# Attention probabilities against values: eight groups of two heads in quarters of the array's columns, in place of four groups of four heads

## What is computed

```python
x = x + _L0_conv_ref(_gn(x), L0_conv_W)
x = x + _L1_conv_ref(_gn(x), w_qkv, b_qkv, rpb, w_proj, b_proj)
...
qkv = (x @ w_qkv + b_qkv).reshape(B, H, W, 3, HEADS, HEAD_DIM)   # 16 heads of 8
for a in range(7):
    for b in range(7):
        logits.append(einsum('bnhwd,bnhwd->bnhw', q, ks) + bias)   # key at the window's (a, b)
attn = softmax(stack(logits))
out = sum over the window of attn * v
return out @ w_proj + b_proj
```

## Time and profile before

| | before |
|---|---|
| median of 3 runs | 1246.21 us (1243.89 to 1247.28) |
| the profiled execution | 1245.71 us |
| its span, first to last instruction | 1243.9 us |
| mean granted TensorE clock | 0.905 of 2.4 GHz |
| busy: TensorE / VectorE / ScalarE / GpSimd | 1097.8 / 885.1 / 666.9 / 594.8 us |

### The profile page before, as it was taken

How to read it: one execution, slowest core, us unless ns; L and a number is a source line. 1 busy time by engine, 2 the same in 40 slices (tenths; PEclk the granted TensorE clock), 3 DMA queues, 4 the chain that set the end, 5 groups by cost and what they waited for, 6 DMA issues and landing times.

```text
span 1243.9 us, 33582 instructions
## 1 busy us (share of the span) xinstructions
PE 1097.8 (88%) x12452; PEld 766.3 (62%) x12452; DVE 885.1 (71%) x2137; ACT 666.9 (54%) x1874; POOL 594.8 (48%) x1279
## 2 busy tenths in 40 slices
PE   3799999946489999999999999999999999999993
PEld 3555555536257676766767666666776667677762
DVE  2522212269778888898888889887888888788881
ACT  2300000061076766868677686766768576676862
POOL 4000000050055757576575766657576665747661
PEclk7599999965588999999999999998999899899995
DMA  9400000034055767677586766757576675858661
GB/s 257 86 26 39 39 26 39 37 86 103 14 129 136 194 124 192 133 170 159 128 195 126 191 131 155 181 124 183 114 199 130 155 171 123 190 110 206 132 155 55
DMA packets 145433, 159.96 MB, mean 129 GB/s; under 512 B 32016, under 2 KB 122736, under 8 KB 145016
## 3 DMA queue, kind: packets, MB, share of 16 engines
q1 hardware_dynamic: 144408, 153.92, 54.1%
q0 software_dynamic: 864, 3.90, 0.9%
HBM read 86.49 MB, written 70.87 MB: 127 GB/s over the span
## 4 chain that ended last, share of the span: by engine, by line
PE 63%; DVE 11%; POOL 10%; DMA 7%; issue 4%; ACT 2%; SPq 1%; POOLq 0%; DVEq 0%; ACTq 0%
PE PS L1128 15%; PE PS L1236 13%; PE PS L1199 11%; PE PS L1220 6%; PE PS L1140 5%; POOL area L635 5%; PE PS L1213 4%; DVE bias L980 4%; PE PS L1181 3%; POOL late L616 3%; POOL halves L613 2%; DVE area L1022 2%; PE PS L1246 2%; DMA area<-x 2%; DMA area<-q_parts 2%
## 5 line engine op out<-in xcount | busy, mean ns | idle before, releaser
L613 POOL TENSOR_TENSOR halves<-masked 128x96 f32<-128x96 f32 (+1 forms) x512 | 203.6, 398 | 304.6 <-DVE masked L1054 264.4
L1236 PE MATMUL PS<-S,VT 128*36 128x96 f32 (+1 forms) x4096 | 286.7, 263 | 32.7 <-ACT S L797 31.6
L1043 DVE TENSOR_TENSOR S<-PS,bias 128x384 f32<-128x384 f32 (+1 forms) x513 | 283.1, 552 | 0.0
L797 ACT ACTIVATE S<-S 128x384 f32<-128x384 f32 (+1 forms) x512 | 270.9, 542 | 2.4 <-DVE S L1043 2.1
L1199 PE MATMUL PS<-area 97*128 97x48 bf16 (+1 forms) x4112 | 256.9, 210 | 15.4 <-DVE S L1043 11.6
L790 ACT ACTIVATE VT<-PS 128x128 f32<-128x128 f32 x449 | 127.3, 284 | 265.5 <-PE PS L1181 262.1
L1236 PEld LDWEIGHTS PS<-S,VT 128*36 128x36 f32 x4096 | 171.8, 116 | 157.7 <-issue 74.2
L1033 DVE TENSOR_REDUCE mcol<-PS 128x6 bf16<-128x480 f32 (+2 forms) x297 | 181.8, 612 | 96.5 <-PE PS L1220 94.8
L1199 PEld LDWEIGHTS PS<-area 97*128 97x128 bf16 x4112 | 185.0, 103 | 98.3 <-DVE S L1043 18.3
L1054 DVE TENSOR_TENSOR masked<-PS,cst 128x192 f32<-128x192 f32 (+1 forms) x512 | 180.6, 353 | 40.7 <-PE PS L1236 35.3
L1128 PE MATMUL PS<-area 128*128 128x392 f32 x576 | 192.5, 497 | 3.8 <-DVE area L922 3.8
(11 more groups left out here) (87 smaller groups left out, 1204.0 us busy)
## 6 DMA issues: line engine op xcount, KB each, us to landing
area<-k_parts SPq DMA_DIRECT2D x33, 1008.0 KB, 8.3
area<-q_parts SPq DMA_DIRECT2D x66, 294.0 KB, 9.6
k_parts<-area SPq DMA_DIRECT2D x34, 504.0 KB, 6.0
...
```

The lines of the kernel that those rows point to most:

```text
L613: nc.gpsimd.tensor_tensor(h, m[:, :, 0:2, :], m[:, :, 2:4, :], ALU.add).then_inc(s["half"], 1)
L797: nc.scalar.activation(S[:, n % 4, 0:cols], S[:, n % 4, 0:cols], ACT.Exp).then_inc(s["probs"], 1)
L1043: nc.vector.tensor_tensor(S[:, n % 4, 0:cols], PS[:, SCORE + n % 2, 0:cols], bias[:, at:at + cols], ALU.add).then_inc(s["biased"], 1)
L1236: last = mm(PS[64 * (g % 2):64 * (g % 2) + VALUE_COLS, SUM + n % 2, at:at + q], VT[:, w % 4, g, :], S[:, n % 4, q * g:q * (g + 1)], start= ...
```

## The change

The 16 heads are now eight groups of two. A group has 16 value columns and 2 columns of ones, 18 in all, and 48 columns of `S`. Group `g` writes partitions 32 * (g % 4) to 32 * (g % 4) + 17, so four quarters of the array's columns are in use in place of two halves, and two groups share each quarter. `weigh` issues eight matmuls of 48 columns in place of four of 96. `select_heads` has two heads per group to choose from and writes 96 columns in place of 192. `add_heads` is one addition of two heads: the first one, `halves` and the semaphore `half` go, and `select_heads` waits for `summed` of the tile before the last instead. The projection weights, the denominators and the mask are laid out for the four quarters, for which four loads of `wproj` become eight, two DMAs of `collect_denominators` become four, and two of `spread_reciprocals` become four; the bytes stay. The order of the steps on every engine stays.

```diff
--- before.py
+++ after.py
@@ -50,7 +50,9 @@
 PEAK_ROW = 2 * HEAD_ROWS
 HEAD_PAIRS = HEADS // 2
 WINDOWS = 14
-VALUE_COLS = 32 + 4
+GROUPS, GROUP_HEADS = 8, 2
+GROUP_DIMS = GROUP_HEADS * HEAD_DIM
+VALUE_COLS = GROUP_DIMS + GROUP_HEADS
 
 X_RING = 4
 OUTER_KINDS = (0, 1, 2, 12, 13)
@@ -165,7 +167,7 @@
 
 
 
-C_ID, C_GROUP, C_HEAD, C_OUT, CONSTS = 0, 128, 256, 272, 276
+C_ID, C_GROUP, C_HEAD, C_OUT, CONSTS = 0, 128, 256, 272, 274
 
 
 BF16_ONE = 0x3F80
@@ -181,8 +183,8 @@
     c[:, C_ID:C_ID + 128] = np.eye(128)
     c[:, C_GROUP:C_GROUP + 128] = p[:, None] // NORM_GROUP == p[None] // NORM_GROUP
     c[:, C_HEAD:C_HEAD + HEADS] = (2 * (p % HEAD_PAIRS) + p // 64)[:, None] == np.arange(HEADS)[None]
-    own = np.where(p % 64 < 32, p % 32 // HEAD_DIM, p % 64 - 32)
-    c[:, C_OUT:C_OUT + 4] = own[:, None] == np.arange(4)[None]
+    own = np.where(p % 32 < GROUP_DIMS, p % 32 // HEAD_DIM, p % 32 - GROUP_DIMS)
+    c[:, C_OUT:C_OUT + GROUP_HEADS] = own[:, None] == np.arange(GROUP_HEADS)[None]
     for a in range(2):
         for n, at, count in bias_kinds(a):
             if n < ROWS_OF_PATCHES:
@@ -242,9 +244,9 @@
         bias = sb("bias", [128, BIAS_COLS])
         biasp = sb("biasp", [128, 2, BIAS_PATCHES, PATCH_KEYS], BF16)
         S = sb("S", [128, 4, 512])
-        VT = sb("VT", [128, 4, 4, VALUE_COLS])
+        VT = sb("VT", [128, 4, GROUPS, VALUE_COLS])
         mcol = sb("mcol", [128, PATCHES], BF16)
-        masked = sb("masked", [128, 2, 256])
+        masked = sb("masked", [128, 2, 128])
         halves = sb("halves", [128, 2, 128])
         packed = sb("packed", [128, PATCHES])
         den = sb("den", [128, 2 * CHUNK_Q])
@@ -307,13 +309,13 @@
 
 
 
-        CREDIT = {"xin_kept": X_RING, "conv_added": 4, "weighted": 4, "scores": 1, "selected": 2, "half": 2,
+        CREDIT = {"xin_kept": X_RING, "conv_added": 4, "weighted": 4, "scores": 1, "selected": 2, 
                   "value_out": 1, "summed": 1, "normed": 1, "out_done": 1}
         EACH = {"misc_in": 20, "misc_out": 20, "rows_in0": 2 * ROWS_IN, "rows_in1": 2 * ROWS_IN, "first_in": 64, "outer_in": 64, "middle_in": 64, "scores": 64, "biased": 64, "probs": 64,
-                "weighted": 64, "selected": 64, "half": 64, "summed": 64, "qbd": 4, "qbd_too": 4, "peak_in": 4 * CHUNK_BANKS,
+                "weighted": 64, "selected": 64, "summed": 64, "qbd": 4, "qbd_too": 4, "peak_in": 4 * CHUNK_BANKS,
                 "peak_out": 4 * CHUNK_BANKS, "value_in": 4 * WINDOWS, "value_out": 4 * WINDOWS,
                 "lead": 6, "rest": 12, "second": 6, "third": 12, "k_stored": 192, "q_stored": 256,
-                "sums_out": 128, "packed_in": 64, "recip": 4, "recip_out": 64, "den_in": 128, "normed": 4,
+                "sums_out": 256, "packed_in": 64, "recip": 4, "recip_out": 64, "den_in": 256, "normed": 4,
                 "xa_in": 32, "xr_in": 32, "residual": 2, "out_done": 32, "xn_ready": 2}
         s = {name: ctx.enter_context(nc.semaphore("s_" + name)) for name in (
             *EACH, "init", "spaces", "weights", "scratch", "warm", "cleared", "x_mid_out", "pool_loaded", "const_in", "loaded",
@@ -330,7 +332,7 @@
         ident, group = cst[:, C_ID:C_ID + 128], cst[:, C_GROUP:C_GROUP + 128]
         MEAN, RSTD = 0, 1
         INITS, SPACES, WEIGHTS = 10, 5, 3
-        SMALL_LOADS, POOL_LOADS = 16 * 5, 16 * (4 + 9 + 2 + 1)
+        SMALL_LOADS, POOL_LOADS = 16 * 5, 16 * (GROUPS + 9 + 2 + 1)
         MISC_IMAGE, MISC_FIRST = 10, 6
         block = ctx.enter_context(nc.Block())
 
@@ -484,14 +486,14 @@
 
                 to = sums[(c + 1) % 2]
                 wait(sp, "summed", TILES * c, j)
-                for g in range(2):
-                    sp.dma_start(to[4 * g:4 * g + 4, :],
-                                 sel[64 * g + 32:64 * g + VALUE_COLS, sel_of(j, c - 1), :, :, :].rearrange("p g q t -> p (g q t)")
+                for g in range(4):
+                    sp.dma_start(to[GROUP_HEADS * g:GROUP_HEADS * (g + 1), :],
+                                 sel[32 * g + GROUP_DIMS:32 * g + VALUE_COLS, sel_of(j, c - 1), :, :, :].rearrange("p g q t -> p (g q t)")
                                  ).then_inc(s["sums_out"], 16)
 
             def pack_denominators(j, c):
                 to = sums[(c + 1) % 2]
-                wait(sp, "sums_out", 32 * (c + 1), j)
+                wait(sp, "sums_out", 64 * (c + 1), j)
                 sp.dma_start(packed[:, :], to.rearrange("h n -> (h n)").rearrange("(p n) -> p n", p=128)
                              ).then_inc(s["packed_in"], 16)
 
@@ -507,9 +509,9 @@
                 to = sums[(c + 1) % 2]
                 wait(sp, "recip_out", 16 * (c + 1), j)
                 wait(sp, "normed", c + 1, j)
-                for g in range(2):
-                    src = to[4 * g:4 * g + 4, :].unsqueeze(1).broadcast_to([4, HEAD_DIM, 2 * CHUNK_Q])
-                    sp.dma_start(den[64 * g:64 * g + 32, :], src).then_inc(s["den_in"], 16)
+                for g in range(4):
+                    src = to[GROUP_HEADS * g:GROUP_HEADS * (g + 1), :].unsqueeze(1).broadcast_to([GROUP_HEADS, HEAD_DIM, 2 * CHUNK_Q])
+                    sp.dma_start(den[32 * g:32 * g + GROUP_DIMS, :], src).then_inc(s["den_in"], 16)
 
             def store(j, i, img):
                 wait(sp, "misc_out", misc_turn(i, 1) + 1, j)
@@ -578,8 +580,8 @@
             for ap, value in ((padded[0], 0.0), (padded[1], 0.0), (den[:, :], 1.0)):
                 nc.gpsimd.memset(ap, value).then_inc(s["cleared"], 1)
             pool.wait_ge(s["cleared"], 1)
-            for g in range(4):
-                pool.dma_start(wproj[64 * (g % 2):64 * (g % 2) + 32, g // 2, :], w_proj[32 * g:32 * g + 32, :]
+            for g in range(GROUPS):
+                pool.dma_start(wproj[32 * (g % 4):32 * (g % 4) + GROUP_DIMS, g // 4, :], w_proj[GROUP_DIMS * g:GROUP_DIMS * (g + 1), :]
                                ).then_inc(s["pool_loaded"], 16)
             for tap in range(9):
                 pool.dma_start(wconv[:, tap, :], conv_w[tap // 3, tap % 3].unsqueeze(0).broadcast_to([CH // NORM_GROUP, NORM_GROUP, CH])
@@ -608,12 +610,8 @@
                 wait(pool, "selected", T + 1, j)
                 if n == 0:
                     wait(pool, "normed", c, j)
-                m = masked[:, n % 2, 0:8 * q].rearrange("p (g h q) -> p g h q", g=2, h=4)
-                h = halves[:, n % 2, 0:4 * q].rearrange("p (g h q) -> p g h q", g=2, h=2)
-                nc.gpsimd.tensor_tensor(h, m[:, :, 0:2, :], m[:, :, 2:4, :], ALU.add).then_inc(s["half"], 1)
-                wait(pool, "half", T + 1, j)
-                h = halves[:, n % 2, 0:4 * q].rearrange("p (g h a t) -> p g h a t", g=2, h=2, a=PATCH)
-                nc.gpsimd.tensor_tensor(sel[:, sel_of(j, c), :, :, t0:t0 + count], h[:, :, 0], h[:, :, 1], ALU.add
+                m = masked[:, n % 2, 0:4 * q].rearrange("p (g h a t) -> p g h a t", g=2, h=GROUP_HEADS, a=PATCH)
+                nc.gpsimd.tensor_tensor(sel[:, sel_of(j, c), :, :, t0:t0 + count], m[:, :, 0], m[:, :, 1], ALU.add
                                         ).then_inc(s["summed"], 1)
 
             def add_residual(j, i):
@@ -787,8 +785,8 @@
                 wait(act, "value_in", w + 1, j)
                 if j is not None:
                     wait(act, "weighted", tiles_until(w - 4), j)
-                nc.scalar.activation(VT[:, w % 4, :, 0:32],
-                                     PS[:, VALUE, 0:128].rearrange("p (g c) -> p g c", g=4),
+                nc.scalar.activation(VT[:, w % 4, :, 0:GROUP_DIMS],
+                                     PS[:, VALUE, 0:128].rearrange("p (g c) -> p g c", g=GROUPS),
                                      ACT.Copy).then_inc(s["value_out"], 1)
 
             def exponentials(j, c, n):
@@ -1048,10 +1046,10 @@
                 q = PATCH * tile_of(c % 2, n)[1]
                 T = TILES * c + n
                 wait(dve, "weighted", T + 1, j)
-                wait(dve, "half", T - 1, j)
-                src = PS[:, SUM + n % 2, 0:8 * q].rearrange("p (g h q) -> p g h q", g=2, h=4)
-                mask = cst[:, C_OUT:C_OUT + 4].unsqueeze(1).unsqueeze(3).broadcast_to([128, 2, 4, q])
-                nc.vector.tensor_tensor(masked[:, n % 2, 0:8 * q].rearrange("p (g h q) -> p g h q", g=2, h=4), src, mask,
+                wait(dve, "summed", T - 1, j)
+                src = PS[:, SUM + n % 2, 0:4 * q].rearrange("p (g h q) -> p g h q", g=2, h=GROUP_HEADS)
+                mask = cst[:, C_OUT:C_OUT + GROUP_HEADS].unsqueeze(1).unsqueeze(3).broadcast_to([128, 2, GROUP_HEADS, q])
+                nc.vector.tensor_tensor(masked[:, n % 2, 0:4 * q].rearrange("p (g h q) -> p g h q", g=2, h=GROUP_HEADS), src, mask,
                                         ALU.mult).then_inc(s["selected"], 1)
 
             def invert(j, c):
@@ -1061,7 +1059,7 @@
 
             def divide(j, c):
 
-                wait(dve, "den_in", 32 * c, j)
+                wait(dve, "den_in", 64 * c, j)
                 wait(dve, "misc_in", misc_project(c - 1) + 1, j)
```

(8 more changed lines are left out.)

## The result

The changed kernel takes **1287.1 us** (median of 3 runs, 1285.91 to 1291.78) against 1246.2: ratio 1.034, 95% interval 1.030 to 1.039, 41 us slower. The forecast was 61 us faster.

A forecast was written before the change was run, and what follows sets the result against it. TensorE (63% of the chain), VectorE and GpSimd were taken to bound different tiles. Gains of 0.1, 1.05, 1.4 and 1.5 make 4.05 us an image, 65 in all, less 3.5 at the end: 1185 us, range 1155 to 1205.

The forecast's parts named there:

- The slack is 5 us: SyncE's query fill in the odd chunk: lands 5 us before the scores need it, so later issue costs nothing.
- SyncE is late: Rival: the odd chunk's query fill lands 1 us too late per image, 1201 us; chance 0.06.
- Weigh: L1236 on TensorE: four rounds of 0.04 us in place of four of 0.08; gain taken as 0.15 us a tile.
- No overlap: Rival: in weigh each record waits for the one before, 0.32 us more a tile, 1326 us; chance 0.09.
- floor per record: Rival: weigh's records take 0.025 us each across quarters, losing 0.08 us a tile, 1226 us; chance 0.09.
- two at a time: Rival: weigh runs eight rounds of 0.04 us and stays at 0.46 us, 1204 us; chance 0.13.
- Select: VectorE's select of heads: 96 columns less save 0.10 us a tile.
- (a): Tiles with only a six-patch bank, 11 an image: VectorE's reduction loop leaves 0.01 us each, 0.1 us.
- The clock: Rival: one more TensorE stretch at 1.2 GHz an image, 1205 us; chance 0.08.
- (d): GpSimd within even chunks: ScalarE's wait of 1.49 us and TensorE's of 1.60 go, 1.5 us an image.
- (c): Tiles 10 to 15 and the next chunk's 0, 14 an image: VectorE's saving of 0.10 us each, 1.4 us.
- (b): Tiles with more TensorE work or a smaller bank, 7 an image: TensorE bounds, 0.15 us each, 1.05 us.

The follow-up runs named there:

- the one-DMA kernel: Changed kernel with 16 partitions a head, so one DMA collects and one spreads in place of four and four: 1249.6 us, 1.0014.
- the runs of 5: Matmuls into unused columns added, twelve tiles: the one-DMA kernel 1252.1, kernel before 1276.0, changed kernel 1290.8 us; only where free: the one-DMA kernel 1245.0, before 1250.6.
- runs 1: SyncE's odd-chunk list reordered, next keys and queries loaded ahead of the first spreading and collecting: changed kernel 1258.6 us, 1.0125; kernel before 0.9996.
- 3: 16 partitions a head, one collecting and one spreading DMA: changed kernel 1249.6 us, 1.0014; kernel before 1252.9 us, 1.0075.
- 6: Even chunk's reciprocals stored and spread earlier: the filled kernel 1257.0 us, 1.0137; changed kernel 1259.9 us, 1.0154; kernel before 0.9993.
- the filled kernel: The one-DMA kernel plus matmuls into unused columns only in tiles where they had cost nothing: 1245.0 us, 0.9977.
- the cut kernel: The one-DMA kernel with weigh cut to its first four groups plus one matmul of 240 columns: 1239.4 us, 0.9961.

## Why the prediction was wrong

**The step that failed: "The slack is 5 us; it falls by 2.2 and by the shorter chunk, some 2, and stays positive. I cost it at nothing."** Three errors are in it. First, 9.6 us is the median landing over both halves of the fill; the scores need the slower half. Issue and landing in that very chunk, before:

```profile
L462 SPq DMA_DIRECT2D area<-q_parts x2: 586/602/617, 601.1 to 601.8; - x2
...
DMA to landing us min/median/max: 8.5/10.3/12.1
```

and the scores for the next chunk stood in the trace at 614.35, not "at about 616":

```profile
614.35 0.49 PE L1199 MATMUL PS<-area 97*128 97x48 bf16 x8 [0.27 <-issue]
```

The half issued last is the slower one: 601.75 + 12.1 is 613.8, so the scores began 0.5 us after it. In none of the 16 odd chunks do they begin less than 0.46 us after the landing, not even where they waited for it, and in the median chunk it is 1.0 us; so the slack was nothing here and some half a microsecond in the median. The kernel before says the same in all its odd chunks: with the fill issued up to 8.5 us into the chunk step 30 takes 1.08 us, and at 8.6 and 9.0 it takes 1.9 and 1.7. Second, I counted only the DMAs' issue time, 2.2 us; the fill came 5.4 us later. The other 3 us are the list of the even chunk, which holds 21.0 us of issues (20.7 before) and did not shrink, so that the reciprocals' round trip moved from the even chunk's cover into the odd chunk's head. Third, the rival "SyncE is late" had the right mechanism with 1 us an image; step 30 alone went from 1.1 to 5.1 and step 31 from 2.2 to 3.5.

By the other terms:

- *Weigh.* Forecast 0.15 to 0.16 us a tile; measured 0.16. The quarters do run four at once: the records start in fours, which was a sign of being right. "No overlap", "floor per record" and "two at a time" are out: sixteen records of 48 columns start within 0.16 us, 0.01 us apart on the mean, where those of L1164 in the earlier trace rows are 0.025 apart, so that floor does not add up across quarters. The Trainium skill (TensorEngine Tiling (Array Packing), Instruction Overhead) asks about 60 cycles of each matmul; this case's traces agree with it for one stream (L1164) and not for four.
- *Select*: 250 ns for 349, as forecast. *Heads*: L613 gone; the remaining addition takes 292 ns, not 337.
- *(a)*, forecast 0.01 a tile. The tiles repeat every 1.49 us against 1.58, so 0.09. The loop of bank and maximum exists and sets the 1.49 us: the reduction of 0.66 ends at 730.33, the bank starts 0.06 behind it, at 730.39, and the next reduction 0.77 behind that, at 731.16. But the weight load of 0.10 us that I put into the loop is not in its way. That the gap was 0.16 before because TensorE was still busy is my reading.
- *Even chunk*: forecast 26.5, measured 26.9. *Odd chunk*: forecast 22.8, measured 29.4; the steps' sum of the one-DMA kernel, which has little of the stall, is 23.7.
- *The clock*, one stretch an image more: there are 19 more stretches in 16 images, so the count was right, by luck: 16 of the 33 begin in step 30, in the wait for the queries, which the rival did not have. And the runs of 5 give the clock some 5 us, not 20.

*(d)* was forecast at 1.5 us an image, on the ground that ScalarE's wait for GpSimd goes and TensorE's behind it with it. Close to half of the first stayed, before and after (from 350 to 1200 us, in total, times and longest):

```profile
ACT area L770 <- POOL area L635: 26.8, 32, 1.5
```

```profile
ACT area L768 <- POOL area L633: 10.9, 15, 0.8
```

TensorE's went from 1.6 to 1.2 us an image. The one-DMA kernel shows the steps with little of the stall: *(c)* and *(d)* together, steps 10 to 16, 26 to 31 and 0, gave 1.1 us where 2.9 were forecast, and the other steps 2.5 where *(a)* and *(b)* had 1.15. That the sum, 3.6, is near the forecast 4.05 is luck: two errors cancel.

So the gain on TensorE and VectorE was there, 3.6 us an image, and none of it could arrive. The change shortened all that stood beside a chain of stores, fills and small DMAs, lengthened that chain, and the chain had 1 us or less to spare. 27 to 37 us of the loss are shown to be SyncE's list (runs 1, 3 and 6, three different ways; 23 to 41 us by their ratios). How the remaining 60 us of forecast gain share out between late fills, instruction loads and the clock stays open: each taken away alone is replaced by the others (5 us for the clock; 10 and 3 for the instructions). Moving the fills or the small DMAs to another engine's queue was not tried. No version that computes all heads beat the kernel before by more than the measurement can tell; the closest is the filled kernel, at 0.9977 [0.9951, 1.0003], and its median, 1245.0, lies 2 us above that of the kernel before run beside it. The one interval below 1 is that of the cut kernel, 0.9961 [0.9927, 0.9994], which leaves half the heads out.
